# Seven places instead of four for the rows on their way to the experts' tiles

## What is computed

```python
xn = _layernorm(x)
x + mamba(xn) + moe(xn)

# mamba: a selective scan over the 2048 positions of each batch
x_in, z = split(xn @ W_in)                       # 512 channels each
u = silu(conv4(x_in) + conv_b)
dt_lr, Bm, Cm = split(u @ W_xproj)               # 16, 16 states, 16 states
delta = softplus(dt_lr @ W_dt + b_dt)
h = exp(delta * A) * h + (delta * u) * B_t       # per channel and state
y = (sum over states of h * C_t + D_skip * u) * silu(z)
y @ W_out

# moe: each of 4096 rows goes to its 2 best of 16 experts
w, e = top2(softmax(xn @ Wr + br)), w / sum(w)
h = gelu(layernorm(xn @ W1[e] + b1[e]) * g1[e] + be1[e])
sum over the 2 of w * (h @ W2[e] + b2[e])
```

## Time and profile before

| | us |
|---|---|
| median of 3 runs | 1147.27 (1146.32 to 1148.31) |
| the profiled execution | 1143.7 |
| its span | 1141.9 |
| DVE busy | 1044.0 (91%) |
| PE busy | 935.8 (82%) |
| ACT busy | 869.0 (76%) |
| POOL busy | 867.7 (76%) |
| mean granted TensorE clock | 0.902 |

### The profile page before, as it was taken

How to read it: one execution, slowest core, us unless ns; L and a number is a source line. 1 busy time by engine, 2 the same in 40 slices (tenths; PEclk the granted TensorE clock), 3 DMA queues, 4 the chain that set the end, 5 groups by cost and what they waited for, 6 DMA issues and landing times.

```text
span 1141.9 us, 16963 instructions
## 1 busy us (share of the span) xinstructions
PE 935.8 (82%) x4570; PEld 638.4 (56%) x4571; DVE 1044.0 (91%) x1308; ACT 869.0 (76%) x1875; POOL 867.7 (76%) x561
## 2 busy tenths in 40 slices
PE   4917775478969999779998999799987999888775
PEld 3404444254556656556566666476655766576554
DVE  7898999799999999897799989989998999999894
ACT  4544787555877789856999789977998699986871
POOL 5058898569767688758878778967977887986895
PEclk9958895588988999879998999889997999999888
DMA  9575558863457434925349543673446542964313
GB/s 298 192 281 206 178 173 281 291 231 98 129 196 228 79 94 104 318 89 121 83 108 303 153 88 84 207 259 74 111 109 240 172 112 62 306 190 107 70 19 65
DMA packets 119367, 185.86 MB, mean 163 GB/s; under 512 B 12012, under 2 KB 104344, under 8 KB 111016
## 3 DMA queue, kind: packets, MB, share of 16 engines
q1 hardware_dynamic: 87120, 144.60, 37.9%
q0 software_dynamic: 19584, 25.26, 12.8%
q10 hardware_dynamic: 12568, 14.93, 4.1%
HBM read 146.34 MB, written 42.60 MB: 165 GB/s over the span
## 4 chain that ended last, share of the span: by engine, by line
PE 37%; ACT 18%; issue 14%; DVE 10%; POOL 10%; DMA 6%; ACTq 3%; SPq 1%; POOLq 0%; DVEq 0%
PE psY L1081 8%; POOL hc L620 6%; PE psC L1219 5%; ACT hb L792 4%; PE psA L1106 4%; DVE hb L1547 4%; PE psC L1169 4%; PE psA L1154 4%; PE psE L1196 3%; ACT hnT L907 3%; DMA xs_d<-xg,slots 2%; PE psA L1098 2%; POOL xs_d L633 2%; POOL out L667 1%; ACT L910 1%
## 5 line engine op out<-in xcount | busy, mean ns | idle before, releaser
L620 POOL TENSOR_TENSOR hc<-hb,Cb 128x1024 f32<-128x1024 f32 x244 | 615.9, 2665 | 109.6 <-PE psY L1081 71.0
L1547 DVE TENSOR_TENSOR_SCAN hb<-hb,carry,psB 128x512 f32<-128x512 f32 x384 | 471.9, 1263 | 11.9 <-ACT hb L792 10.8
L1081 PE MATMUL psY<-ident,hc 128*128 128x128 f32 x2048 | 309.0, 293 | 75.2 <-POOL hc L620 48.3
L1081 PEld LDWEIGHTS psY<-ident,hc 128*128 128x128 f32 x2048 | 258.5, 151 | 188.5 <-issue 108.3
L792 ACT ACTIVATE hb<-delta,aneg 128x512 f32<-128x512 f32 x512 | 352.4, 716 | 6.5 <-issue 2.6
L1536 DVE TENSOR_TENSOR psB<-Bb,psU 128x512 f32<-128x512 f32 x512 | 325.1, 679 | 1.5 <-DMA Bb<-bc_d 1.4
L667 POOL DMA_INDIRECT out<-yo,idx x80 | 128.8, 1610 | 53.9 <-DMA out<-yo,idx 13.8
L1547 DVE TENSOR_TENSOR_SCAN hb<-hb,psB 128x512 f32<-128x512 f32 x128 | 149.3, 1201 | 2.2 <-ACT hb L792 2.2
L1106 PE MATMUL psA<-ux,dgw 128*128 128x512 f32 x232 | 111.3, 595 | 3.5 <-ACT ux L734 3.5
L633 POOL DMA_INDIRECT xs_d<-xg,slots x64 | 69.0, 1078 | 36.6 <-DMA xg<-xn_d 20.0
L1219 PE MATMUL psC<-w2r,hnT 128*128 128x256 f32 x320 | 87.8, 422 | 0.0
(11 more groups left out here) (230 smaller groups left out, 1175.0 us busy)
## 6 DMA issues: line engine op xcount, KB each, us to landing
Bb<-bc_d SPq DMA_DIRECT2D x32, 1024.0 KB
Cb<-bc_d SPq DMA_DIRECT2D x32, 1024.0 KB, 5.1
w1r<-w1c_d SPq DMA_DIRECT2D x80, 256.0 KB
w2r<-in_L_ffn_W SPq DMA_DIRECT2D x80, 256.0 KB
xg<-xs_d SPq DMA_DIRECT2D x20, 516.0 KB
xg<-xn_d SPq DMA_DIRECT2D x64, 128.0 KB
Bb<-in_L_attn_x SPq DMA_DIRECT2D x8, 512.0 KB, 9.3
xn_d<-hb SPq DMA_DIRECT2D x8, 512.0 KB, 8.7
```

The lines of the kernel that those rows point to most:

```text
L620: pool.tensor_tensor(hc[:, k:k + 2, :], hb[:, g % HR:g % HR + 2, :], Cb[:, n:n + 2, :], ALU.mult).then_inc(s_g, 1)
L1081: mm = pe.matmul(y[:, tt * P:(tt + 1) * P], hc[:, g % GR, tt * P:(tt + 1) * P], ident[:, :], start=False, stop=(n == NS - 1), is_transpose ...
L1547: dve.tensor_tensor_scan(h, h, psB[g % 2][:, :], first, ALU.mult, ALU.add).then_inc(s_scan, 1)
```

## The change

There are seven places, `NPLACE = 7`. Places 0 to 3 are those of `xg`; places 4 to 6 are 258 columns each of `hnT`, seen flat. Put j uses place j % 7, and each place has its own two semaphores (`s_scl`, `s_sc`). Seven loads and seven metas are issued at the start in place of four, load j and meta j wait for put j - 7, and SP takes up load j at the unit of put j - 7. `load_group(0)` waits for all seven places. The units of the puts and metas stay as they are.

```diff
--- before.py
+++ after.py
@@ -122,6 +122,8 @@
 PUT0 = -1
 PUT_NUM = 7
 PUT_DEN = 5
+
+NPLACE = 7
 META_LEAD = 1
 
 GS = [93, 112, 132, 152, 172, 193, 212, 232, 248, 268, 289, 313, 332, 353, 377, 396, 414, 432, 451, 468]
@@ -336,7 +338,9 @@
         bsum = om[0:E, 3, 0:1]
         wcen = [w1r[:, a, :, :] for a in range(2)] + [w2r[:, j, :, :] for j in range(GT)]
         unread = ygT[:, :, :].rearrange("p (k a) b -> p k (a b)", k=KC)
-        xsrc = xg
+        hnT_flat = hnT[:, :, :, :].rearrange("p a b c -> p (a b c)")
+
+        place = [xg[:, r, :] for r in range(GT)] + [hnT_flat[:, r * DW:(r + 1) * DW] for r in range(NPLACE - GT)]
 
         psB = [psum(f"psB{i}") for i in range(2)]
         psU = psum("psU")
@@ -377,8 +381,8 @@
         s_cm, s_cen, s_cst = sem("s_cm"), sem("s_cen"), [sem(f"s_cst{k}") for k in range(CEN_N)]
 
         s_meta = sem("s_meta")
-        s_scl = [sem(f"s_scl{k}") for k in range(4)]
-        s_sc = [sem(f"s_sc{k}") for k in range(4)]
+        s_scl = [sem(f"s_scl{k}") for k in range(NPLACE)]
+        s_sc = [sem(f"s_sc{k}") for k in range(NPLACE)]
         s_xg, s_w1, s_w2, s_bi, s_acc = sem("s_xg"), sem("s_w1"), sem("s_w2"), sem("s_bi"), sem("s_acc")
         s_t1, s_m1, s_msq, s_mve, s_mrs, s_mh, s_t2, s_mn, s_mg, s_m2, s_pad, s_idx = (sem(n) for n in (
             "s_t1", "s_m1", "s_msq", "s_mve", "s_mrs", "s_mh", "s_t2", "s_mn", "s_mg", "s_m2", "s_pad", "s_idx"))
@@ -463,14 +467,15 @@
 
             def load_rows(j):
                 i = j // 2
-                if j >= 4:
-                    sp.wait_ge(s_sc[j % 4], 16 * (j // 4))
-                sp.dma_start(xsrc[:, j % 4, 0:D], xn_d[i * P:(i + 1) * P, :]).then_inc(s_scl[j % 4], 16)
+                r = j % NPLACE
+                if j >= NPLACE:
+                    sp.wait_ge(s_sc[r], 16 * (j // NPLACE))
+                sp.dma_start(place[r][:, 0:D], xn_d[i * P:(i + 1) * P, :]).then_inc(s_scl[r], 16)
 
             def load_group(g):
                 if g == 0:
-                    for r in range(4):
-                        sp.wait_ge(s_sc[r], 16 * (NPUT // 4))
+                    for r in range(NPLACE):
+                        sp.wait_ge(s_sc[r], 16 * len(range(r, NPUT, NPLACE)))
                     sp.wait_ge(s_zero, 16 * NPAD)
                 else:
                     sp.wait_ge(s_t1, 2 * g)
@@ -526,7 +531,7 @@
             load_bc(0, 0)
             sp.wait_ge(s_w["bst"], 16 * 6)
             sp.wait_ge(s_route, 1)
-            for j in range(4):
+            for j in range(NPLACE):
                 load_rows(j)
             for q in range(1, NS // NQ):
                 load_bc(0, q)
@@ -540,8 +545,8 @@
                     if c + 1 < NC:
                         for q in at(c, "bc_load", s):
                             load_bc(c + 1, q)
-                    for j in range(4, NPUT):
-                        if max(put_unit(j - 4), 0) == G:
+                    for j in range(NPLACE, NPUT):
+                        if max(put_unit(j - NPLACE), 0) == G:
                             load_rows(j)
                     for g, off in groups_at(G):
                         for _ in moe("load", off):
@@ -628,11 +633,12 @@
 
             def put_rows(j):
                 i, k = divmod(j, 2)
-                pool.wait_ge(s_scl[j % 4], 16 * (j // 4 + 1))
+                r = j % NPLACE
+                pool.wait_ge(s_scl[r], 16 * (j // NPLACE + 1))
                 pool.wait_ge(s_meta, j + 1)
                 pool.indirect_dma_start(
                     out=xs_d[:, :], out_offset=bass.IndirectOffsetOnAxis(ap=slots[:, k, i:i + 1], axis=0),
-                    in_=xsrc[:, j % 4, :], in_offset=None).then_inc(s_sc[j % 4], 16)
+                    in_=place[r], in_offset=None).then_inc(s_sc[r], 16)
 
             def put_zeros(k):
 
@@ -858,9 +864,9 @@
                 i, k = divmod(j, 2)
                 if j == 0:
                     act.wait_ge(s_route, 1)
-                elif j >= 4:
-                    act.wait_ge(s_sc[j % 4], 16 * (j // 4))
-                act.activation(xsrc[:, j % 4, D:DW], meta[:, k, i, :], ACT.Copy).then_inc(s_meta, 1)
+                elif j >= NPLACE:
+                    act.wait_ge(s_sc[j % NPLACE], 16 * (j // NPLACE))
+                act.activation(place[j % NPLACE][:, D:DW], meta[:, k, i, :], ACT.Copy).then_inc(s_meta, 1)
 
             def load_cen(e):
                 if e == 0:
```

## The result

| | before | with the change |
|---|---|---|
| median of 13 runs, us | 1148.31 (1142.81 to 1157.08) | 1138.76 (1134.20 to 1142.63) |
| span of the profiled execution, us | 1141.9 | 1137.0 |
| DVE busy, us | 1044.0 (91%) | 1044.7 (92%) |

The ratio of the change to before is 0.9913, with a 95% interval from 0.989 to 0.9935: 7.5 to 12.6 us faster of 1147.3. The two profiled executions differ by less, 4.9 us of span, so their rows can't be added up to the difference of the medians. DVE's work is the same to 0.7 us; what went is waiting.

A forecast was written before the change was run, and what follows sets the result against it. DVE, busy 91% of the span, was taken to bound the kernel. The terms -5.9 - 2.5 + 1.4 = -7.0 us took the median from 1147.27 to 1140.3 us, with a range from 1134.6 to 1146.5.

The forecast's parts named there:

- First gap: DVE's 8.04 us wait before 215.30 for ACT's softplus, held up at meta 41, shrinks to 2.1 us: -5.9 us.
- Second gap: DVE's 2.47 us wait before 235.04 goes, as ACT no longer stands 4.06 us for put 41: -2.5 us.
- POOL's waits: POOL's 20.0 us of waits for loaded rows vanish but for 1 or 2 us, adding nothing to DVE's gain.
- The three loads at the start: Three more loads ahead of the Bb quarters lengthen that 1.44 us wait by at most 2.4 us, hidden: 0.
- DMA give-back: From 183 to 239 us busy DMA engines may return 0 to 3.9 us of the 8.4; 1.4 taken.
- The -4.5 us: Sum if, by the Trainium skill alone, more transfers in flight on the same 16 DMA engines add no bandwidth.
- Rival A: The stall only moves: metas 44 to 47 wait for puts still under the copy; gain about 3 us, 1144; chance 0.14.
- Rival C: Slower: DVE and POOL collide on line 1556, 2.18 us per full meeting, up to 1153.4 us; chance 0.10.
- 13.1 us for six new meetings: Cost if all six DVE multiplications on line 1556 at or after 198.53 newly meet POOL's: 1153.4 us.

The follow-up runs named there:

- the earlier delta: The change with DVE's second softplus delta of chunk 0 moved from behind unit 59 to behind unit 57: 1141.27 us, ratio 0.9922 to the kernel before.
- the old metas: The change with seven places and loads seven apart, but each meta write waiting for the put four earlier: 1144.64 us, ratio 0.9984 to the kernel before.
- the old loads: The change with seven places and metas seven apart, but each load waiting for the put four earlier: 1142.32 us against 1146.33 before, ratio 0.9967.
- the early copy: Copy of x to out issued in the prologue; with the change's seven places 1136.21 us against 1147.39 for the kernel before, ratio 0.9894.

## Why the prediction was right

The forecast was 1140.3 us, 7.0 below the median; measured is 1138.76, with 7.5 to 12.6 us of gain. Sign and mechanism held, and the size is a little short. One step was wrong, POOL's, and chance helped to cover it. By its steps:

- **First gap, -5.9 us: right.** 8.04 us became 2.14 where 2.1 was worked out, and what is left is the chain of DVE, PE and ACT, as the earlier delta showed by removing it. The metas alone bring this term.
- **Second gap, -2.5 us: right in the first profile, half right in the second.** It is gone in the first and 1.40 us in the second. With the old metas it was 1.0 us, and with the old loads 1.41. All three profiles with 1.40 or 1.41 us there (old loads, earlier delta, the change once more) have a wait for sums just ahead of it: what is left comes with a late POOL.
- **POOL's waits vanish but for 1 or 2 us, and DVE does not feel them: wrong.** 11.3 us stayed (9.91 + 1.43). The step looked at load 39 only and left the copy at 191.24. ACT, freed of waits at metas, issues it at 188.51, and load 40 falls in behind it. Nor was it free for DVE: it cost 2.2 us at pair 64 in the first profile and 2.6 us of waits in the second, where the same seven places with the early copy took 32.7 us from unit 64 to 80, and the change 34.9 and 35.5.
- **The three loads at the start, 0: right.** The wait for the Bb quarter grew from 1.44 to 2.41 us, the gap behind it shrank from 4.42 to 3.46, and unit 16 came 0.3 us later.
- **DMA give-back, +1.4 us: 2.2 us, and by another path.** No wait of DVE for Bb grew after 190 us. What was given back came by POOL, 2.2 us in the first profile. That the sum held so well is luck: 1.7 us were made good at pair 78, which took 2.97 us before and 1.23 with the change, and which the sum did not have. From unit 48 to 96 the first profile won 8.0 us: 5.9 + 2.5 - 2.2 + 1.7 = 7.9. In 191 to 197 us the engines moved 475 GB/s, against 382:

```profile
191.00:197.00 6.00, 2.61 (x12) 2.62 (x13) 5.97 (x5) 5.65 (x17) 5.50 (x4) 0.50 1.24 475
```

  A share near one was no fixed rate, as the row of 233 to 239 us had hinted. The Trainium skill says that transfers interleave on the same 16 engines whichever engine started them (DMA: Bandwidth & Descriptors, Issuing engines are not separate DMA queues). Load 40 agrees, which on SP's queue took 19.8 us behind ACT's copy. The -4.5 us that the prediction drew from it was too little: the measured gain is 7.5 us at the least.
- **Rival A** (the stall moves) came true for POOL and, with five places, for ACT. **Rival C** (meetings) came true once, at pair 64, and was paid back once, at pair 78. The prediction's 13.1 us for six new meetings was too much, since pair 78 had already met POOL before the change, at 255.45 (2.97 us). It does not decide the sign.

The rest of the measured gain is not settled. The first profile of before had no meeting at pair 10; the second did, and took 3.3 us longer there. It stands in three of the four profiles with metas four apart and pair 10 on DVE (three kernels, before twice), and in none of the eight with metas five or seven apart (two of these took 1.72 us there). The longer distance may thus spare DVE the meeting in some executions, which would explain a median gain above that of the two gaps; this is argued from twelve profiles, not shown.

## What to carry to other kernels

When a queue stands at a buffer's release, ask what is queued behind it that the bound engine needs: 40 us of ACT's waits cost DVE 8, all in two places where a softplus stood behind. Do not take a wait for free because the bound engine has not felt it yet: POOL's cost nothing that showed before, and 2.2 to 2.6 us once DVE was earlier. Depth cures a late landing only with a margin, since an engine that is freed issues its own transfers earlier and moves the collision; taking the large transfer out of the stretch cured all but 1.1 us of it with four buffers. And before a few microseconds between two profiles are read, profile the same kernel twice.

## What the runs showed of the hardware

- Behind or beside a 4 MB copy from DRAM to DRAM, transfers of other queues land late: puts of 0.13 MB in 13 us (before, put 37) and 16 us (five places, put 35), where one in a calm stretch took 2.3; and a load of 0.13 MB issued 0.2 us behind it took 19.8 us, for a median of 2.7.
- DVE's product with two SBUF inputs took 1.23 us alone and 3.4 to 4.2 us where it met the whole of POOL's of the same kind. It waits out what is left of POOL's instruction: in all thirteen profiles, each of DVE's products of pairs that took 1.48 us or more ended 1.08 to 1.10 us after the product, or the du, that POOL was making. At pair 10 the order of two starts decides. DVE met POOL in the three profiles in which it began 0.3 to 0.6 us after POOL's put, and not in the nine in which it began before it. With the change DVE began at 100.14:

```profile
100.23 2.02 POOL L639 DMA_INDIRECT xs_d<-hnT,slots  x1 [0.17 <-issue]
102.27 2.35 POOL L625 TENSOR_TENSOR hc<-hb,Cb 128x1024 f32<-128x1024 f32 x1
```

  and with the old metas at 100.36, during the put. DVE's product then took 3.96 us:

```profile
99.83 1.01 POOL L639 DMA_INDIRECT xs_d<-hnT,slots  x1 [0.17 <-issue]
100.87 2.36 POOL L625 TENSOR_TENSOR hc<-hb,Cb 128x1024 f32<-128x1024 f32 x1
```

- One kernel, executed twice, had TensorE's low clock at two places of its program 6 us apart, and the two executions differ by 2.9 us in the 16 units there.
